# The tail of a transformer layer: a list level for the last three token tiles, and chunk sums by tensor_reduce

## The reference

```python
x = x + attention(layernorm(x))                   # causal, one head of width 1024, scale 1/32
h = layernorm(x)
s = softmax(h @ gate_w.T)                         # 8 experts
top_s, sel = top_k(s, 2)
y = silu(h @ w1[e]) * (h @ w3[e]) @ w2[e]         # for each of a token's two experts e
x = x + sum over the two choices of top_s * y
```

## Time and profile before

| | |
|---|---|
| median of 3 runs | 241.94 us (239.41 to 242.28) |
| the profiled execution | 241.13 us, its span 239.4 us |
| busy in the span | TensorE 228.4 us (95%), VectorE 186.4 (78%), ScalarE 145.9 (61%), GpSimd 163.3 (68%) |
| mean granted clock of TensorE | 0.998 |
| last instruction of TensorE, VectorE | 235.4, 237.0 us |
| chunk adds of L1366 | 16, 684 ns each |

### The profile page before, as it was taken

How to read it: one execution, slowest core, us unless ns; L and a number is a source line. 1 busy time by engine, 2 the same in 40 slices (tenths; PEclk the granted TensorE clock), 3 DMA queues, 4 the chain that set the end, 5 groups by cost and what they waited for, 6 DMA issues and landing times.

```text
span 239.4 us, 6515 instructions
## 1 busy us (share of the span) xinstructions
PE 228.4 (95%) x1822; PEld 209.5 (88%) x1823; DVE 186.4 (78%) x848; ACT 145.9 (61%) x391; POOL 163.3 (68%) x204
## 2 busy tenths in 40 slices
PE   7989999999999999999999999989999999999953
PEld 6978888898889867787999999889999999999953
DVE  2489898879897789977898799757766666699935
ACT  2267777777877766854699565646565656556100
POOL 6523337788888888868587787777777777778500
PEclk9999999999999999999999999999999999999999
DMA  7999801101111111123134336434333333796474
GB/s 227 305 322 331 224 5 35 46 26 45 37 47 35 48 45 35 48 67 102 37 88 106 95 92 154 120 90 123 94 107 96 106 99 97 232 344 188 134 246 148
DMA packets 31946, 28.89 MB, mean 121 GB/s; under 512 B 4136, under 2 KB 26544, under 8 KB 31920
## 3 DMA queue, kind: packets, MB, share of 16 engines
q1 hardware_dynamic: 26448, 19.39, 29.5%
q0 software_dynamic: 4096, 8.53, 10.5%
q10 hardware_dynamic: 1376, 0.66, 0.9%
HBM read 16.34 MB, written 12.22 MB: 119 GB/s over the span
## 4 chain that ended last, share of the span: by engine, by line
PE 83%; DMA 4%; DVE 3%; POOL 3%; ACT 2%; issue 2%; POOLq 1%; DVEq 0%; SPq 0%
PE scores L725 13%; PE turned L725 12%; PE scores L596 12%; PE weighed L652 12%; PE scores L746 6%; PE turned L622 6%; PE weighed L746 3%; PE mixed L746 3%; PE mixed L611 3%; PE mixed L610 3%; DMA XX<-choice_rows 2%; POOL expert_rows L503 2%; DVE X L1366 2%; PE scores L742 2%; DMA TL<-L_attn_w_o 2%
## 5 line engine op out<-in xcount | busy, mean ns | idle before, releaser
L514 POOL DMA_INDIRECT choice_rows<-ysb,ycol x64 | 64.8, 1013 | 19.5 <-issue 12.5
L503 POOL DMA_INDIRECT expert_rows<-rows,slots x64 | 64.4, 1007 | 18.2 <-issue 12.7
L863 ACT ACTIVATE Wt<-W 128x512 f32 x71 | 44.1, 626 | 15.7 <-issue 15.7
L725 PE MATMUL scores<-xT,Wt 128*128 128x128 f32 x288 | 38.2, 276 | 1.1 <-DVE xT L1197 1.1
L596 PE MATMUL scores<-XX,TL 128*128 128x512 f32 (+3 forms) x96 | 38.1, 506 | 0.2 <-ACT TL L836 0.2
L652 PE MATMUL weighed<-TL,PT 128*128 128x136 f32 x272 | 37.0, 281 | 0.4 <-DVE X L987 0.3
L725 PE MATMUL turned<-xT,Wt 128*128 128x128 f32 x280 | 37.1, 275 | 0.0
L725 PEld LDWEIGHTS scores<-xT,Wt 128*128 128x128 f32 x288 | 35.0, 192 | 1.3 <-DVE xT L1197 1.3
L652 PEld LDWEIGHTS weighed<-TL,PT 128*128 128x128 f32 x272 | 33.6, 190 | 1.1 <-issue 0.8
L725 PEld LDWEIGHTS turned<-xT,Wt 128*128 128x128 f32 x280 | 34.1, 192 | 0.0
L975 DVE TENSOR_REDUCE negmax<-scores 128x1 f32<-128x128 f32 (+7 forms) x32 | 23.5, 735 | 5.5 <-PE scores L596 5.5
(11 more groups left out here) (184 smaller groups left out, 462.9 us busy)
## 6 DMA issues: line engine op xcount, KB each, us to landing
xt<-expert_rows SPq DMA_DIRECT2D x71, 66.0 KB
XX<-choice_rows SPq DMA_DIRECT2D x16, 256.0 KB
W<-L_ffn_w SPq DMA_DIRECT2D x2, 1024.0 KB, 8.9
out<-X SPq DMA_DIRECT2D x9, 128.0 KB
X<-L_attn_in_features SPq DMA_DIRECT2D x2, 512.0 KB, 7.4
expert_rows<-rows,slots POOLq DMA_INDIRECT x64, 2.3
choice_rows<-ysb,ycol POOLq DMA_INDIRECT x64, 2.4
out<-X ACTq DMA_DIRECT2D x5, 128.0 KB
```

What stands on the lines that cost most here:

```text
L503: nc.gpsimd.indirect_dma_start(xs, bass.IndirectOffsetOnAxis(ap=slots[:, u, k:k + 1], axis=0), rows[:, u % ROWS_RING, k, :], None).then_in ...
L514: nc.gpsimd.indirect_dma_start(yb, bass.IndirectOffsetOnAxis(ap=ycol[:, q, 0:1].bitcast(u32), axis=0), ysb[:, q, :], None).then_inc(y_out[ ...
L725: mm(bank[2 + j % RING][:, c * P:(c + 1) * P], Wt[:, j % RING, c * P:(c + 1) * P], xT[:, j % RING, :], start=True, stop=True)
L863: copy(Wt[:, j % RING, :], W[:, ds(w * (SET // WIDE), SET)], ACT.Copy).then_inc(Wt_rdy, 1)
```

## The change

- **List.** A fourth level is added: the first 29 token tiles, counted apart from the last three (SOWN = 3). `ranks` gets two more small products and `places` one more copy of counts; `list_rest` works on 32 segments instead of 24. FAR's bound LATER goes from 64 to 63 tiles.
- **Sowing.** STORED becomes 65 and BY_PE 6; a sown tile takes three products instead of four, `picks` compares with 384 places instead of 512, and `clear` goes: the first product starts the accumulation. In the last three steps `pair` comes before `sow`.
- **Stores.** The hardware loop covers tiles 32 to 47; tiles 48 to 64, 17 of them, are issued from straight code without pacing.
- **Early chunks.** X and the region of TL become one tensor `three` of three layers; chunks 0 to 4 are fetched into layers 1 and 2, in the layout of X (rows of 512 bytes at a stride of 544; chunks 1 to 4 in four transfers instead of two), without a wait for an earlier sum. `add_both` sums half a chunk in one tensor_reduce over the three layers, innermost, into a new tensor `done`, from which the output is written. They stand where the adds stood.
- **Late chunks.** Chunks 5 and 6 are fetched after 63 stores. The last chunk is fetched after 65, one choice on the sync queue and one on ScalarE's. VectorE finishes the last three results first, then adds chunks 5 and 6, then the PSUM tiles, then the last chunk in four instructions of half a chunk and one choice each.

```diff
-FAR, LATER = 6, 64
-LEVELS = (HALF, FAR, len(GROUPS) - 1)
+FAR, LATER = 6, 63
+SOWN = 3
+LEVELS = (HALF, FAR, len(GROUPS) - 1, len(GROUPS) - 1)
...
-BY_PE = 7
-STORED = NT - BY_PE
+STORED = (K * P * (N_TILES - SOWN) + E * (P - 1)) // P
+BY_PE = NT - STORED
...
-ZF = 4
+ZF = 3
...
+REST_OF = (STORED // OUT_LANES, STORED % OUT_LANES)
...
-        X = sb("X", [P, N_TILES, VG])
+        three = sb("three", [P, K + 1, N_TILES, VG])
+        X = three[:, 0, :, :]
+        done = sb("done", [P, N_EARLY, FIN, D])
...
-        place_of_tok = sb("place_of_tok", [P, FIN, P])
+        place_of_tok = sb("place_of_tok", [P, SOWN, P])
         lowi, lowf = sb("lowi", [P, BY_PE], u32), sb("lowf", [P, BY_PE])
-        pick = [B_[:, h, n * FIN * P:(n + 1) * FIN * P] for B_ in (Pr, PT) for h in range(2) for n in range(2)]
+        pick = [B_[:, h, n * SOWN * P:(n + 1) * SOWN * P] for B_ in (Pr, PT) for h in range(2) for n in range(2)]
...
+        def sown_at(i):
+
+            return (ACC[0], 0) if i < SOWN - 2 else (ACC[1], (i - SOWN + 2) * D)
...
+        def stores_in(eng, t0, t1):
+
+            for q in range(OUT_LANES):
+                if len(range(q, t1, OUT_LANES)) > len(range(q, t0, OUT_LANES)):
+                    eng.wait_ge(y_out[q], 16 * len(range(q, t1, OUT_LANES)))
+
+        def fetch_last(eng, k):
+
+            eng.dma_start(yf[:, LAST - N_EARLY, k, :, :], yv[:, k, LAST, :, :]).then_inc(yf_in[LAST], 16)
+
+        def write_last(eng, h):
+
+            n, z = pieces(LAST)[h]
+            eng.wait_ge(last1, h + 1)
+            eng.dma_start(ov[:, n:n + z, :], X[:, n:n + z, 0:D]).then_inc(out_done, 16)
...
             def fetch(c):
-                wait(sp, sum1, c - ZF + 1)
                 for k in range(K):
-                    sp.dma_start(yf[:, c % ZF, k, :, :], yv[:, k, c, :, :]).then_inc(yf_in[c % ZF], 16)
+                    if c < N_EARLY:
+                        for n, z in pieces(c):
+                            i = 0 if n == CHUNKS[c][0] else 2
+                            sp.dma_start(three[:, 1 + k, n:n + z, 0:D], yv[:, k, c, i:i + z, :]).then_inc(yf_in[c], 16)
+                    else:
+                        sp.dma_start(yf[:, c - N_EARLY, k, :, :], yv[:, k, c, :, :]).then_inc(yf_in[c], 16)
 
             def write(c):
+                sp.wait_ge(sum0, c + 1)
                 sp.wait_ge(sum1, c + 1)
                 for n, z in pieces(c):
-                    sp.dma_start(ov[:, n:n + z, :], X[:, n:n + z, 0:D]).then_inc(out_done, 16)
+                    i = 0 if n == CHUNKS[c][0] else 2
+                    sp.dma_start(ov[:, n:n + z, :], done[:, c, i:i + z, :]).then_inc(out_done, 16)
...
-            for q in range(OUT_LANES):
-                sp.wait_ge(y_out[q], 16 * len(range(q, LATER, OUT_LANES)))
-            for c in range(N_EARLY, NF):
+            stores_in(sp, 0, LATER)
+            for c in range(N_EARLY, LAST):
                 fetch(c)
-
-            sp.wait_ge(sum2, 1)
-            n, z = pieces(LAST)[0]
-            sp.dma_start(ov[:, n:n + z, :], X[:, n:n + z, 0:D]).then_inc(out_done, 16)
+            stores_in(sp, LATER, STORED)
+            fetch_last(sp, 0)
+            write_last(sp, 0)
...
-            with pool.Fori(NT0 // OUT_LANES, (NT - 1) // OUT_LANES) as r:
+            with pool.Fori(NT0 // OUT_LANES, REST_OF[0] - 1) as r:
                 for q in range(OUT_LANES):
                     store(r, q)
+            for t in range((REST_OF[0] - 1) * OUT_LANES, STORED):
+                store(t // OUT_LANES, t % OUT_LANES)
...
+                if gr == NG - 1:
+
+                    for b in range(n - SOWN + 1):
+                        mm(RANKS[:, (n + 1) * E:(n + 2) * E], onesb[:, :], counted[:, gr, b, :], start=b == 0,
+                           stop=b == n - SOWN)
...
-            def clear():
-
-                pe.wait_ge(y_rdy, LAST_TURN - LAG)
-                for a in ACC:
-                    mm(a[:, 0:2 * D], onesb[:, :], counted[:, 0, 0:1, :].to_broadcast([P, 2 * D // E, E]),
-                       start=True, stop=False)
-
             def sow(t):
 
                 n = t - STORED
                 pe.wait_ge(y_rdy, t + 1)
                 pe.wait_ge(pick_rdy, n + 1)
-                for i in range(FIN):
-                    o = mm(ACC[i // 2][:, i % 2 * D:(i % 2 + 1) * D], pick[n][:, i * P:(i + 1) * P], ysb[:, t % OUT_LANES, :],
-                           start=False, stop=n == BY_PE - 1 and i % 2 == 1)
-                    if n == BY_PE - 1 and i % 2 == 1:
-                        o.then_inc(sown_mm, 1)
+                for i in range(SOWN):
+                    a, at = sown_at(i)
+                    o = mm(a[:, at:at + D], pick[n][:, i * P:(i + 1) * P], ysb[:, t % OUT_LANES, :],
+                           start=n == 0 and at == 0, stop=n == BY_PE - 1, skip_group_check=True)
+                if n == BY_PE - 1:
+                    o.then_inc(sown_mm, 1)
...
-                if static and t == STORED + SOW_LAG:
-                    clear()
...
-                sow(t - 2)
                 pair(*divmod(t + LAG, LANES), w[LIST0 + t % LANES])
+                if t - 2 >= STORED:
+                    sow(t - 2)
...
+            stores_in(act, 0, STORED)
+            fetch_last(act, 1)
...
-                    link(v.tensor_copy(cnt[:, LEVELS.index(gr), :], RANKS[0:1, n * E:(n + 1) * E]))
+                    link(v.tensor_copy(cnt[:, NL - 1 if gr == NG - 1 else LEVELS.index(gr), :],
+                                       RANKS[0:1, n * E:(n + 1) * E]))
+                if gr == NG - 1:
+                    link(v.tensor_copy(cnt[:, NL - 2, :], RANKS[0:1, (n + 1) * E:(n + 2) * E]))
...
+            def add_both(c, h):
+
+                a, apart = CHUNKS[c]
+                n = a + h * apart
+                dve.wait_ge(yf_in[c], 16 * K * len(pieces(c)))
+                v.tensor_reduce(done[:, c, 2 * h:2 * h + 2, :], three[:, :, n:n + 2, 0:D].rearrange("p k t d -> p t d k"), AX.X,
+                                ALU.add).then_inc([sum0, sum1][h], 1)
...
-                        add_choice(ADD_AT.index(t - k), k)
+                        add_both(ADD_AT.index(t - k), k)
...
-            for t in range(NT - LAG, NT):
-                out_pair(*divmod(t + LAG, OUT_LANES))
-                if t == NT - LAG:
-                    for k in range(K):
-                        add_choice(N_EARLY, k)
-            for c in range(N_EARLY + 1, NF):
+            for t in range(NT, NT + LAG):
+                out_pair(*divmod(t, OUT_LANES))
+            for c in range(N_EARLY, LAST):
                 for k in range(K):
                     add_choice(c, k)
+
+            n1 = N_TILES - SOWN
+            dve.wait_ge(sown_mm, 1)
+            for i in range(SOWN - 2):
+                v.tensor_tensor(X[:, n1 + i, 0:D], X[:, n1 + i, 0:D], ACC[0][:, i * D:(i + 1) * D],
+                                ALU.add).then_inc(sum2, 1)
+            v.tensor_tensor(X[:, N_TILES - 2:, 0:D], X[:, N_TILES - 2:, 0:D],
+                            ACC[1][:, 0:2 * D].rearrange("p (n d) -> p n d", d=D), ALU.add).then_inc(sum2, 1)
+
+            dve.wait_ge(yf_in[LAST], 16 * K)
             for h, (n, z) in enumerate(pieces(LAST)):
-                dve.wait_ge(sum1, NF)
-                dve.wait_ge(sown_mm, h + 1)
-                v.tensor_tensor(X[:, n:n + z, 0:D], X[:, n:n + z, 0:D],
-                                ACC[h][:, 0:z * D].rearrange("p (n d) -> p n d", d=D),
-                                ALU.add).then_inc(sum2, 1)
+                at = n - CHUNKS[LAST][0]
+                dve.wait_ge(sum2, min(SOWN - 2, 1) if h == 0 else SOWN - 1)
+                v.tensor_tensor(X[:, n:n + z, 0:D], X[:, n:n + z, 0:D], yf[:, LAST - N_EARLY, 0, at:at + z, :],
+                                ALU.add).then_inc(last0, 1)
+                dve.wait_ge(last0, h + 1)
+                v.tensor_tensor(X[:, n:n + z, 0:D], X[:, n:n + z, 0:D], yf[:, LAST - N_EARLY, 1, at:at + z, :],
+                                ALU.add).then_inc(last1, 1)
```

More of the change, by code:

```diff
@@ L236, in build @@
             sem("y_zero"), sem("low_rdy"), sem("lowf_rdy"), sem("pick_rdy"), sem("sown_mm"))
-        sum2 = sem("sum2")
+        sum2, last0, last1 = sem("sum2"), sem("last0"), sem("last1")
         assert NF - N_EARLY == LAG
-        yf_in = [sem(f"yf_in{j}") for j in range(ZF)]
+        yf_in = [sem(f"yf_in{c}") for c in range(NF)]
         sum0, sum1, out_done = sem("sum0"), sem("sum1"), sem("out_done")
@@ L299, in build @@
         assert RANK_LAG <= LANES
-        assert LATER == STORED and BY_PE <= len(pick) and FIN * P == 512
+        assert BY_PE <= len(pick) and STORED // OUT_LANES == (NT - 1) // OUT_LANES
         LAST = NF - 1
@@ L934, in _ @@
                     act.dma_start(ov[:, n:n + z, :], X[:, n:n + z, 0:D]).then_inc(out_done, 16)
-            act.wait_ge(sum2, 2)
-            n, z = pieces(LAST)[1]
-            act.dma_start(ov[:, n:n + z, :], X[:, n:n + z, 0:D]).then_inc(out_done, 16)
+            write_last(act, 1)
         @block.vector
```

16 lines of the change are left out of this document (9 added, 7 removed).

## The result

The changed kernel takes 242.90 us at the median of 16 executions (242.18 to 243.96); the kernel before 241.19 (16 executions, 239.40 to 243.44). The ratio is 1.0088, with a 95% interval of 1.0065 to 1.0111: slower, by 1.6 to 2.7 us, and not by the 8.6 us of the forecast. The time lies inside the range of 240.0 to 253.5, which reached so far down only to hold the first rival. The profiled execution took 243.23 us, its span is 241.5.

The account below looks back on a forecast made before the run. TensorE paces the middle; the tail is a chain of stores, fetches and VectorE adds. Forecast: 246.4 + 0.7 (list) + 1.0 (clock) = 248.1 us span against 239.4, stated as 250.5 us at the median, range 240 to 253.5.

Parts of the forecast that it names:

- rival one: Early chunks' reduces on VectorE run at full rate, 0.86 us instead of 1.66: 241.6 us at the median; chance 0.22.
- The price of the reduce: Early chunks on VectorE: two cycles an element for 768 elements, 1.73 us each, 1.66 until the next instruction.
- third reading: Pricing spaced elements on VectorE: L1035 set against L1068 puts the spacing's cost at 21 ns for 40 elements.
- rival two: Early chunks' reduces cost something in between, 1.0 to 1.35 us, if only buffer jumps cost: 243 to 246.5; chance 0.08.
- Rival one's break: Reduce price on VectorE below which the change is not slower: 0.89 us a reduce.
- VectorE's chain: From 208.99 through ten reduces to the last ysb, VectorE sets the pace after t=62: 239.0 us.
- TensorE's wait: Near the last pairs TensorE does almost nothing from 228.2 to 233.2, 5 us idle.
- The stores: GpSimd's stores: five holds by adds, 2.0 us in all, go; unpacing gives nothing; the 65th starts at 233.7.
- Fetches: Early fetches don't show; late ones issue from 233.6, the last chunk lands at 241.5, and VectorE never waits.
- Sowing: TensorE: 18 products instead of 28 and no clearing, 2.4 us less, hidden in the waits for ysb.
- The list: 1 x 1280 operations hide in VectorE's spare time; held stores lengthen TensorE's stall before 156.30: 0.7 us (0 to 1).
- The clock: After TensorE's idle time near 231 the clock may fall to 1.2 GHz: 1.0 us (0 to 4).

Follow-up runs that it names:

- experiment 2: Changed kernel with nine of its ten reduces given other shapes: spacing from 16 bytes up costs 0.08 to 0.09 us; contiguous takes 0.95 us.
- experiment 6: Changed kernel with the stores of tiles 48 to 63 back in the paced hardware loop: 242.53 us, ratio 1.0100 to the kernel before.
- Experiment 1: Changed kernel with two adds in place of each early-chunk reduce, all else kept: 240.62 us, ratio 0.9984 to the kernel before.
- experiment 5: Changed kernel with three list levels again and four sown token tiles instead of three: 243.90 us, ratio 1.0096 to the kernel before.
- c_both: Changed kernel with three list levels and the fifth chunk's reduces moved behind the last results: 241.56 us, ratio 1.0020 to the kernel before.
- c_move: Changed kernel with the fifth chunk's reduces between the last three ysb, its write after the late fetches: 241.15 us, ratio 0.9990 to the kernel before.
- experiment 4: Kernel before with only a fourth list level, counted and never used: 242.63 us, ratio 1.0067.
- c_both_adds: Changed kernel with three list levels, the fifth chunk's sums moved, and two adds per reduce: 239.73 us, ratio 0.9933 to the kernel before.
- a_adds: Changed kernel with two adds for each of the ten reduces, all else kept: 240.62 us, ratio 0.9984 to the kernel before.
- b_reduce: Kernel before with only the early sums changed (three layers, split fetches, ten reduces, separate output): 244.08 us, ratio 1.0138.

## Why the prediction was half right

The forecast was 250.5 and the time 242.9: a slowdown of 8.6 us was forecast and one of 1.6 to 2.7 measured, so the direction was right and the size was not. Its parts, in its order.

**The price of the reduce: wrong, and the step that failed.** "I therefore take two cycles an element" gave 1.66 us occupied; it is 0.945. The two rows behind it, L1035 and L1174, differ from their neighbours by 45 to 50 ns at 40 elements. I read that as a cycle per element; experiment 2 finds 80 to 90 ns at 768. The prediction's own third reading, 21 ns against L1068, spoke against the rule and was passed over. A difference at one size can't tell a fixed cost from one per element, and both rows had the same size. In the sum this is 7.15 us of the 8.6 forecast. The truth lies between rival one (0.86, 241.6 us) and rival two (1.0 to 1.35, 243 to 246.5). Rival one's break, "0.89 us a reduce", fits: 0.945 is above it, and the kernel is slower. No run has a reduce near 0.89 to try it.

**VectorE's chain: right.** With 0.945 in place of 1.66 the ten reduces give back 7.15 us. Tile 64's ysb is then done at 233.2 - 7.15 = 226.05, with the list's 0.7 at 226.75 (226.87 in the trace), and the sum comes to 246.4 - 7.15 + 0.7 + 1.0 = 240.95 for a span of 241.5. In the profiled execution the list took 1.1 instead of 0.7, which is most of the rest.

**TensorE's wait: right in kind.** It waits for ysb, 2.51 us rather than 5.

**The stores: right.** From 205 us on all last 0.95 to 0.96, and the last ones wait for ysb; unpacing does nothing that shows (experiment 6). That 2.0 us of holds go was right, and worth nothing by itself, since the stores then wait for VectorE. Experiment 1 brings the holds back with the adds.

**Fetches: right.** VectorE never waits for an early chunk or a late one; they are issued behind the last early write, as forecast (227.84 against a forecast of 233.6, which is 226.45 with the quicker reduce and 227.15 with the list).

**Sowing, "hidden in the waits for ysb": in part wrong.** It was put at nothing in the sum. Of the 2.4 us of TensorE 0.86 show in the changed kernel (experiment 5 against 6), since products of sowing stand in the last three steps, where VectorE waits for TensorE; the waits for ysb that I had in mind came earlier. Where VectorE has no waits (c_both against c_move) some 0.2 show. The larger saving, 0.8 us of places tables on VectorE, was in the forecast's chain.

**The list: right number, wrong path, so luck.** 0.7 (0 to 1) was said, the traces' means differ by 0.7, and the isolated run says 0.7 to 2.5 us. But it was to come from a stall that grows by 0.66 behind held stores, while the operations "hide in the spare 0.59 us of the steps". The stall was 0.66 instead of 1.15, and the nine steps ahead of it took 1.3 to 1.8 us more: the operations don't hide (experiment 4).

**The clock: right in kind.** In the profiled execution it falls to 1.2 GHz for some 3.4 us, which cost 1.4 us of its tail; over the 16 executions it is some 0.4 us on average instead of 1.0, if the nine with a lower mean are those with the fall.

**The account.** Alone, the reduces cost 3.3 us (1.6 to 5.0) and the list 1.6 (0.7 to 2.5), and the change as a whole 2.1 (1.6 to 2.7). The rest of it thus gives back about 2.8, or 2.0 if the reduces are taken at the 2.5 of experiment 1. Of that, less sowing, with its tables on VectorE, is 1.1 to 1.9 by the traces, the late order up to 1.0 in one trace and nothing in the medians. How the remainder splits was not settled: the intervals of the two alone are as wide as it.

**What stays open.** Why c_both_adds beats c_both by 0.9% when its one trace is no shorter; and what decides whether the clock falls after the same 2.51 us.

## What to carry to other kernels

When an instruction's price must be read from other rows, take two sizes of the same form: one size can't part a start-up cost from a cost per element, and at 20 times the size the two readings differ by 20 times. A fused instruction that does the work of two must be counted against the time that the two really occupy (0.60 us each here, not their 0.68), and against the gap in the step where it stands. Before making work on an engine quicker or fewer, look where others wait for it: moving two of the ten reduces by some 5 us, with the write of their chunk, gave back as much as adds in place of all ten did. And one trace is one execution: the changed kernel's had a fall of the clock in it that others of the same tail did not have, and set beside them it would have hidden three quarters of what a seventh sown tile costs.

## What the hardware did that I had not expected

A reduce over spaced elements costs 80 to 90 ns more for 768 elements from 16 bytes to 17 KB apart, and nothing at 8 bytes; the number of results doesn't matter. A store issued by GpSimd is lengthened by a two-operand add on a single partition as well: 2.08 and 1.98 us beside the 1 x 1280 adds of the list, and never beside a reduce. The same idle time of TensorE, 2.51 us, was followed by a fall of the granted clock in one trace and by none in three. And the spread between executions differs much from kernel to kernel: 239.4 to 243.4 us before and 238.6 to 242.4 for a_adds, against 242.2 to 244.0 after; it isn't the adds alone, since b_reduce, with reduces, has 242.2 to 245.7. Why was not tried.
